# Reordering one attention round across four engines, and the handover from attention to the expert stage

## What is computed

```python
q = layernorm(x) @ Wq + bq;  k = ctx @ Wk + bk;  v = ctx @ Wv + bv      # head width 32, ctx has 722 rows
scores = q @ k.T / sqrt(512)
scores = (scores - mean) / (std(scores, ddof=1) + 1e-8)                # per row
scores = scores + where(mask, -1e-32, 0)
x = x + tanh(g_xattn) * (tile(softmax(scores) @ v, 16) @ Wout + bout)

probs = softmax(layernorm(x) @ router_w.T)                             # 8 experts
weights, indices = top_k(probs, 2);  weights = weights / (weights.sum() + 1e-6)
h = silu(layernorm(x) @ w13[e, :, :1024]) * (layernorm(x) @ w13[e, :, 1024:])
x = x + tanh(g_ffn) * sum_k weights[k] * (h @ w2[indices[k]])
```

## Time and profile before

| what | value |
|---|---|
| median of 3 runs | 438.82 us (436.67 to 439.89) |
| the profiled execution, its own time | 437.29 us |
| its span, first to last instruction | 435.7 us |
| attention, handover: up to the first expert matmul | 131.08 us |
| expert stage and end | 304.6 us |
| mean granted clock of TensorE | 0.928 |

### The profile page before, as it was taken

The page is one execution under the profiler, slowest core; times in us unless marked ns, Lnnn a source line. Parts: engine busy times, 40 slices in busy tenths (PEclk is TensorE's granted clock), DMA queues, the critical chain, the costliest instruction groups (busy, mean ns, idle before and its releaser), DMA issues.

```text
span 435.7 us, 7132 instructions
## 1 busy us (share of the span) xinstructions
PE 372.8 (86%) x1984; PEld 279.5 (64%) x1985; DVE 231.4 (53%) x512; ACT 189.0 (43%) x314; POOL 124.7 (29%) x214
## 2 busy tenths in 40 slices
PE   2979999763009999999899999999999999999990
PEld 2335444441007788888687888888888888888870
DVE  2227777756840277547975135663951873665120
ACT  1124334434621276257863126734752852673120
POOL 2313454454132123130404303133133140431301
PEclk9989889965558999999999999999999999999996
DMA  7977879712019467638898104872772775200201
GB/s 256 364 237 246 303 256 392 241 51 57 0 41 407 180 186 273 214 68 289 306 350 275 36 12 103 287 265 48 270 260 94 227 230 197 48 24 6 48 0 16
DMA packets 17554, 78.01 MB, mean 179 GB/s; under 512 B 3618, under 2 KB 4770, under 8 KB 10372
## 3 DMA queue, kind: packets, MB, share of 16 engines
q1 hardware_dynamic: 11060, 66.79, 43.3%
q0 software_dynamic: 4720, 7.78, 9.0%
q10 hardware_dynamic: 1760, 3.28, 2.3%
HBM read 71.20 MB, written 7.54 MB: 181 GB/s over the span
## 4 chain that ended last, share of the span: by engine, by line
PE 64%; DMA 9%; DVE 8%; issue 7%; POOL 6%; ACT 2%; DVEq 1%; POOLq 1%; ACTq 0%
PE scp L459 19%; PE turnB L439 17%; PE turnA L439 17%; DMA xg<-xn_d,gidx 5%; DMA ent_next<-lists_d 3%; PE kvp L446 3%; PE kvp L308 3%; PE scp L426 2%; POOL lists_d L968 1%; DVE w13l L785 1%; DVE x L749 1%; DVE bn L752 1%; POOL rs L948 1%; PE turnA L294 1%; PE turnA L364 1%
## 5 line engine op out<-in xcount | busy, mean ns | idle before, releaser
L785 DVE TENSOR_TENSOR w13l<-stage,w13h 128x1024 fp32r<-128x1024 f32 x64 | 75.8, 1218 | 3.9 <-ACT w13h L562 3.3
L562 ACT ACTIVATE w13h<-stage 128x1024 fp32r<-128x1024 f32 x64 | 64.5, 1053 | 0.1
L439 PE MATMUL turnA<-w13h,xTh 128*128 128x512 f32 x128 | 51.4, 401 | 1.6 <-DVE xTl L868 1.6
L439 PE MATMUL turnB<-w13h,xTh 128*128 128x512 f32 x128 | 51.9, 405 | 0.0
L459 PE MATMUL scp<-w2h,hTh 128*128 128x512 f32 x128 | 51.8, 404 | 0.0
L439 PE MATMUL turnA<-w13l,xTh 128*128 128x512 f32 x128 | 51.1, 399 | 0.0
L439 PE MATMUL turnA<-w13h,xTl 128*128 128x512 f32 x128 | 51.0, 398 | 0.0
L439 PE MATMUL turnB<-w13l,xTh 128*128 128x512 f32 x128 | 50.5, 395 | 0.0
L439 PE MATMUL turnB<-w13h,xTl 128*128 128x512 f32 x128 | 50.5, 395 | 0.0
L459 PE MATMUL scp<-w2l,hTh 128*128 128x512 f32 x128 | 50.2, 392 | 0.0
L459 PE MATMUL scp<-w2h,hTl 128*128 128x512 f32 x128 | 49.8, 389 | 0.0
(11 more groups left out here) (162 smaller groups left out, 612.7 us busy)
## 6 DMA issues: line engine op xcount, KB each, us to landing
stage<-in_w_dram SPq DMA_DIRECT2D x48, 1024.0 KB, 5.0
ctx_t<-in_ctx_dram SPq DMA_DIRECT2D x8, 1444.0 KB, 8.8
x_t<-in_x_dram SPq DMA_DIRECT2D x8, 200.0 KB
xT_t<-in_xT_dram SPq DMA_DIRECT2D x8, 200.0 KB, 9.6
out_dram<-x ACTq DMA_DIRECT2D x8, 200.0 KB
xn_d<-xn ACTq DMA_DIRECT2D x8, 200.0 KB
stage<-in_wout_dram SPq DMA_DIRECT2D x1, 1024.0 KB, 11.7
ent_next<-lists_d POOLq DMA_DIRECT2D x17, 1.0 KB, 2.0
```

The source lines that it names most:

```text
L439: mm = pe.matmul(region, xp[:, c, :], wp[:, q, c, :], start=(c == 0 and i == 0), stop=(c == HC - 1 and i == 2))
L562: act.activation(dst, src, ACT.Copy).then_inc(S["w_hi"], 1)
L785: dve.tensor_tensor(lo, raw, hi.bitcast(F32), ALU.subtract).then_inc(S["w_lo"], 1)
```

## The change

- ScalarE does the exponential and the four copies for TensorE first in a round. The store of x2, its normalisation and the exponential of the logits come after them.
- The score's standard deviation is made on GpSimd alone, in four operations; the three of VectorE are gone. The sum `taken` also goes from VectorE to GpSimd, and `choose` compares both experts in one operation without the cast. `ltop` gets two buffers.
- On GpSimd the two list scatters of a round stand last, behind `sigma`, and wait for no earlier scatter.
- On VectorE `make_weights` moves one round on, and `ln1_stats` moves ahead of `fix_query`.
- ScalarE and VectorE count `attn_done` ahead of the first 8 splits. VectorE's last split of expert 0 moves behind `x_lo(0)`. GpSimd fetches tile 0 from row 0, without waiting for `tiles_ready` and without reading `tile_row`.
- TensorE gets two waits, in `heads` and in `outputs`, on work of the batch before.

```diff
         ln2 = sb(a, "ln2", [SQ, 2])
         rs2 = sb(a, "rs2", [SQ, 3])
-        ltop = sb(a, "ltop", [SQ, 8])
+        ltop = [sb(a, f"ltop{i}", [SQ, 8]) for i in range(2)]
...
                 pe.wait_ge(S["v_made"], b + 1)
                 pe.wait_ge(S["vsum_set"], b + 1)
                 pe.wait_ge(S["q_fixed"], 2 * min(b + 3, NB))
+                if b >= 1:
+                    pe.wait_ge(S["lg_made"], b)
                 for j in range(KJ):
                     for half in range(2):
...
                 pe.wait_ge(S["head_copied"], b + 1)
                 pe.matmul(l9, headT[:], wx9[:], start=True, stop=True).then_inc(S["low_done"], 1)
                 pe.wait_ge(S["v_made"], min(b + 2, NB))
+                if b >= 1:
+                    pe.wait_ge(S["x2_ready"], b)
                 pe.matmul(outp[0:SQ, :], headT[:], wsum[:], start=True, stop=True).then_inc(S["out_done"], 1)
 
...
 
+            def store_x2(b):
+                act.wait_ge(S["x2_ready"], b + 1)
+                act.dma_start(out[b], x2[b % 2][:]).then_inc(S[f"out_put{b % 2}"], 16)
...
@@ -564,26 +571,22 @@
             for i in ROUNDS:
                 if live(i - 1):
                     softmax_exp(i - 1)
-                if live(i - 2):
-                    act.wait_ge(S["x2_ready"], i - 1)
-                    act.dma_start(out[i - 2], x2[i % 2][:]).then_inc(S[f"out_put{i % 2}"], 16)
                 if live(i):
                     copy_kv(i)
                 if live(i - 1):
                     copy_probT(i - 1)
-                if live(i - 2):
-                    normalise2(i - 2)
-                    logit_exp(i - 2)
-                if live(i - 1):
                     copy_head(i - 1)
                 if live(i + 1):
                     copy_qT(i + 1)
                 if i == 0:
                     wsum_steps()
-                if i == NB + 1:
-                    for unit in range(0, 2 * NQ):
-                        split_hi(0, unit, None)
+                if live(i - 2):
+                    store_x2(i - 2)
+                    normalise2(i - 2)
+                    logit_exp(i - 2)
             act.drain().then_inc(S["attn_done"], 1)
+            for unit in range(0, 2 * NQ):
+                split_hi(0, unit, None)
 
 
             def x_hi(t):
@@ -699,16 +702,6 @@
                 dve.wait_ge(S["sstat"], 2 * (b + 1))
                 dve.bn_aggr(lns[:], bns[:].rearrange("p a b -> p (a b)")).then_inc(S["s_aggr"], 1)
 
-            def finish_sigma(b):
-                dve.wait_ge(S["sig_root"], b + 1)
-                if b >= 1:
-                    dve.wait_ge(S["exp_done"], b)
-                dve.tensor_scalar(sig[:, 3:4], sig[:, 0:1], (SK / (SK - 1)) ** 0.5, SIGMA_EPS, ALU.mult, ALU.add).then_inc(S["sig_sum"], 1)
-                dve.wait_ge(S["sig_sum"], b + 1)
-                dve.reciprocal(sig[:, 1:2], sig[:, 3:4]).then_inc(S["sig_rec"], 1)
-                dve.wait_ge(S["sig_rec"], b + 1)
-                dve.tensor_scalar(sig[:, 2:3], lns[:, 0:1], sig[:, 1:2], -1.0, ALU.mult, ALU.mult).then_inc(S["sig_ready"], 1)
-
             def raw_logits(b):
                 dve.wait_ge(S["low_done"], b + 1)
...
 
             def choose(b):
                 dve.wait_ge(S["lg_made"], b + 1)
-                if b >= 1:
-                    dve.wait_ge(S["lexp_done"], b)
-                    dve.wait_ge(S["nlmax_done"], b)
-                dve.max(ltop[:], lg[b % 2][:]).then_inc(S["lmax_done"], 1)
+                if b >= 2:
+                    dve.wait_ge(S["lexp_done"], b - 1)
+                    dve.wait_ge(S["nlmax_done"], b - 1)
+                dve.max(ltop[b % 2][:], lg[b % 2][:]).then_inc(S["lmax_done"], 1)
                 dve.wait_ge(S["lmax_done"], b + 1)
-                dve.max_index(pidx[:], ltop[:], lg[b % 2][:]).then_inc(S["pidx_done"], 1)
+                dve.max_index(pidx[:], ltop[b % 2][:], lg[b % 2][:]).then_inc(S["pidx_done"], 1)
                 dve.wait_ge(S["pidx_done"], b + 1)
-                dve.tensor_copy(idxf[:], pidx[:, 0:2]).then_inc(S["idx_cast"], 1)
-                dve.wait_ge(S["idx_cast"], b + 1)
                 if b == 0:
                     dve.wait_ge(S["iotas_made"], 1)
-                for k in range(2):
-                    dve.tensor_scalar(hot[:, k, :], e_num[:], idxf[:, k:k + 1], None, ALU.is_equal).then_inc(S["hot_made"], 1)
-                dve.wait_ge(S["hot_made"], 2 * (b + 1))
+                dve.tensor_tensor(hot[:], e_num[:].unsqueeze(1).to_broadcast([SQ, 2, E]),
+                                  pidx[:, 0:2].unsqueeze(2).to_broadcast([SQ, 2, E]), ALU.is_equal).then_inc(S["hot_made"], 1)
+                dve.wait_ge(S["hot_made"], b + 1)
                 if b >= 1:
                     dve.wait_ge(S["rank_done"], b)
+                    dve.wait_ge(S["taken_made"], b + 1)
                 dve.tensor_tensor(both[:], hot[:, 0, :], hot[:, 1, :], ALU.add).then_inc(S["both_made"], 1)
-                dve.wait_ge(S["both_made"], b + 1)
-                dve.wait_ge(S["taken_made"], b + 1)
-                dve.tensor_tensor(taken[:, b + 1, :], taken[:, b, :], both[:], ALU.add).then_inc(S["taken_made"], 1)
 
             def add_attention(b):
@@ -807,11 +796,15 @@
                 if live(i - 2):
                     choose(i - 2)
                     add_attention(i - 2)
+                if live(i - 3) and i <= NB + 1:
+                    make_weights(i - 3)
+                if live(i + 2) and i >= 1:
+                    ln1_stats(i + 2)
                 if live(i + 1):
                     fix_query(i + 1)
                 if live(i):
                     make_values(i)
-                if live(i + 2):
+                if live(i + 2) and i < 1:
                     ln1_stats(i + 2)
                 if live(i):
                     score_stats(i)
@@ -819,14 +812,8 @@
                     wsum_steps()
                 if live(i - 2):
                     make_places(i - 2)
-                    make_weights(i - 2)
                 if live(i - 1):
                     raw_logits(i - 1)
-                if live(i):
-                    finish_sigma(i)
-                if i == NB + 1:
-                    for unit in range(0, 2):
-                        split_lo(0, unit)
 
             dve.wait_ge(S["cnt_done"], 1)
             dve.wait_ge(S["iotas_made"], 1)
@@ -849,10 +836,10 @@
             dve.wait_ge(S["tilerow_done"], 1)
             dve.scalar_tensor_tensor(out=tile_row[:], in0=t_num[0:1, :], scalar=float(P), in1=scp[0:1, 0:TILES],
                                      op0=ALU.mult, op1=ALU.add).then_inc(S["tiles_ready"], 1)
-            for unit in range(2, 2 * NQ):
+            make_weights(NB - 1)
+            dve.drain().then_inc(S["attn_done"], 1)
+            for unit in range(0, 2 * NQ):
                 split_lo(0, unit)
-            dve.drain().then_inc(S["attn_done"], 1)
-
 
 
...
@@ -903,9 +890,9 @@
                 split(6, 7)
                 split(8, 9)
 
-            for unit in (8, 9):
-                split_lo(0, unit)
+            split_lo(0, 8)
             x_lo(0)
+            split_lo(0, 9)
             with dve.Fori(0, E - 1) as e:
                 t0, t1 = tiles_of(dve, e)
...
@@ -949,13 +936,21 @@
                 pool.wait_ge(S["rstd2"], b + 1)
                 pool.tensor_scalar(rs2[:, 1:2], ln2[:, 0:1], rs2[:, 0:1], -1.0, ALU.mult, ALU.mult).then_inc(S["nmean2"], 1)
                 pool.wait_ge(S["lmax_done"], b + 1)
...
+                pool.tensor_scalar(rs2[:, 2:3], ltop[b % 2][:, 0:1], rs2[:, 0:1], -1.0, ALU.mult, ALU.mult).then_inc(S["nlmax_done"], 1)
 
             def sigma(b):
                 pool.wait_ge(S["s_aggr"], b + 1)
                 if b >= 1:
-                    pool.wait_ge(S["sig_sum"], b)
-                pool.tensor_tensor(sig[:, 0:1], lns[:, 1:2], half[:, 1:2], ALU.pow).then_inc(S["sig_root"], 1)
+                    pool.wait_ge(S["exp_done"], b)
+                link(pool.tensor_tensor(sig[:, 0:1], lns[:, 1:2], half[:, 1:2], ALU.pow))
+                link(pool.tensor_scalar(sig[:, 3:4], sig[:, 0:1], (SK / (SK - 1)) ** 0.5, SIGMA_EPS, ALU.mult, ALU.add))
+                link(pool.tensor_tensor(sig[:, 1:2], sig[:, 3:4], half[:, 2:3], ALU.pow))
+                pool.tensor_scalar(sig[:, 2:3], lns[:, 0:1], sig[:, 1:2], -1.0, ALU.mult, ALU.mult).then_inc(S["sig_ready"], 1)
+
+            def count_taken(b):
+                pool.wait_ge(S["both_made"], b + 1)
+                pool.wait_ge(S["taken_made"], b + 1)
+                pool.tensor_tensor(taken[:, b + 1, :], taken[:, b, :], both[:], ALU.add).then_inc(S["taken_made"], 1)
 
             def scatter(b):
...
                 pool.wait_ge(S["lists_set"], 16)
                 for k in range(2):
-                    if b >= 1:
-                        pool.wait_ge(S[f"lists_put{k}"], 16 * b)
                     pool.indirect_dma_start(lists_d, bass.IndirectOffsetOnAxis(place[:, b, k:k + 1], 0),
```

(19 more changed lines are left out.)

8 lines of the change are left out of this document (3 added, 5 removed).

## The result

Before 438.26 us (median of 4 runs, 436.67 to 439.89), changed 422.64 us (median of 4, 421.65 to 423.76): a ratio of 0.9644, 95% interval 0.9594 to 0.9694, faster. The forecast was 422. The profiled execution of the changed kernel took 421.67, its span is 420.1, its mean granted clock 0.948; before it was 437.29, 435.7 and 0.928. The four runs of the changed kernel lie in two pairs, near 421.7 with a mean clock of 0.948 and near 423.7 with 0.936, so a median of a few runs can move by a microsecond without any edit.

The account below looks back on a forecast made before the run. Ahead of the first expert matmul, attention's rounds, the last batch and the handover bound the kernel, with GpSimd narrowly the new bound of a round. Gains of 7.6, 3.1 and 4.8 sum to 15.5: forecast 422 us, range 417.5 to 429.

Parts of the forecast that it names:

- The first matmul carries the end: From the first expert matmul on nothing changes, so the end moves with it: 115.6 in place of 131.08, 15.5 earlier.
- Rounds, 7.6 gained: Attention's five rounds: one of 7.3, then four of 7.6 bound by GpSimd, in place of 9.06; batch 7's projection at 74.9.
- the clock rival: Attention's rounds: TensorE's clock falls low, 450.5 us; chance 0.03 for slower, 0.05 for about half of it, some 436.
- Last batch, 3.1 gained: Batch 7, projection to logits: shorter waits before the exponential and for copies put the logits at 88.3 in place of 98.99.
- To the last scatter: Batch 7's logits to its second list scatter: start at 99.7 in place of 110.87, with 1.2 for contention with VectorE's splits.
- Handover, 4.8 gained to the request: Attention to experts: earlier counts and no table read put tile 0's list request at 104.5 in place of 120.00.
- From the request to the first matmul 11.08 stays: Tile 0's list request to the first expert matmul: the 11.08 us there was to remain unchanged.
- The splits had cover from TensorE: Handover: the weight splits end 4 to 5 us before TensorE would wait for them.
- The rounds give less: Rival, attention's rounds: in-order queue waits make a round 8.6, batch 7's projection 78.9, time 426; chance 0.15.
- The lists landed in 3.15: Rival, handover: lists land late, in 7.8, with dear port and request, 5.7 more, 427.5 us; chance 0.06.
- The lists' waits: List scatters: only one wait for an earlier scatter ever held GpSimd, 2.06, so dropping them alone gives next to nothing.

Follow-up runs that it names:

- sigma_back: The changed kernel with the deviation finished by three small operations on VectorE again, last in its round, after one power on GpSimd: 422.8 us, ratio 0.965.
- hold_gidx: The changed kernel with VectorE's first long split waiting until GpSimd has made the indices of tile 0: 421.28 us, ratio 0.9638.
- splits_last: The changed kernel with both long splits of VectorE moved behind `x_lo(0)`: 420.51 us, ratio 0.9602.
- before_act: The kernel before with ScalarE's new order and TensorE's two waits alone: 439.79 us, ratio 1.0049.

## Why the prediction was right

**The first matmul carries the end.** Right: 15.07 earlier there, 15.62 in the profiled executions, and 304.1 for the rest.

**Rounds, 7.6 gained.** Measured 7.61 between the projections, batch 7's at 74.65 (forecast 74.9). The sum of GpSimd's loop, 7.57, was nearly right: deviation to deviation is 8.06, 7.73, 7.03 and 8.24 where it carries scatters, a mean of 7.77, and sigma_back shows that this loop and not TensorE's makes the last beat, and 7.5 of the one ahead of it. It was not 7.3 and then four of 7.6 but three of 7.3, then 8.03 and 7.70: the exponential came 1.94 after its statistics ahead of the first scatters and 2.70 in the round behind them, so GpSimd's lateness first used up the slack. The 7.61 is closer than it deserves: 0.2 of it is a projection 2 that began at 36.95 and not 37.16 (batch 7's would be 74.86), and with the fourth round at 7.51 the rounds would have been half a microsecond shorter. The scatter pair cost 3.0 to 3.3 with its issue time, forecast 2.85. Statistics to exponential was 2.7 rather than 2.1 in the round shown, because GpSimd was still at `rs` when the statistics came. The lower clock in the old rounds was not named as a source of the gain; it was contained in the 9.06 from which it was counted. The argument against the clock rival, that the clock was low only where TensorE waited for the last batch, was a misreading: it was 0.72 in two stretches of the rounds.

**Last batch, 3.1 gained.** Measured 3.13 (16.52 to 13.39), logits at 88.04 (forecast 88.3). The sum is right and its terms are not: projection to statistics took 7.05 (forecast 6.6), because x and with it the statistics waited for the store of x2, which ScalarE's new order starts late and for which the prediction had no term; the exponential came 1.95 after them (2.05) and the logits 4.39 after that (4.75). That these errors cancel is luck.

**To the last scatter.** Forecast 97.2 and 99.7 for its two starts; measured 97.00 and 98.83, with 1.5 more in the pair's lengths than the 0.99 each of the earlier trace rows. I had taken 1.2 between the ends 0 and 2.3. The rule of the Trainium skill that one of the two blocks the other ("SBUF — State Buffer", Who interferes with whom) agrees with these rows. Its inference that descriptor generation escapes under a `tensor_tensor` does not hold for the indirect DMAs, by the 1.53 and 1.97 here and the gather of 2.49 in hold_gidx against 1.09. For the direct DMA that requests the list it is not contradicted: 0.63 at 104.23, in the middle of the splits, and 0.62 at 120.00 before, between two of them. Whether it is the reading of places and indices that is held up was not tested.

**Handover, 4.8 gained to the request.** Measured 4.82 (logits to request 21.01, then 16.19); the request at 104.23, forecast 104.5. Here too two errors cancel. From the landing of the last scatter to the request the prediction took 0.7, with 1.6 as the dear end; it was 2.25 (101.98 to 104.23), because GpSimd's own drain of 1.38, which was off the chain while VectorE's splits ended last, now stands on it and had no term. Against that the second scatter began 0.87 earlier than forecast and landed in 3.15 in place of 4.1.

**"From the request to the first matmul 11.08 stays"** is the term that was off: 11.78. `gidx` took 2.34 in place of 0.65 and the gather 1.09 in place of 2.19. I had priced VectorE's hold-up on the scatters and not on the two steps behind them, and in the kernel before one of the two, the gather, already had it. The splits had cover from TensorE, as said, but they cost GpSimd: splits_last gives 2.1 back.

**Rivals.** *The rounds give less* needed 41.7 for the five rounds; they took 37.70. Its counter-argument, that the layer norm's inputs are ready before GpSimd comes to them, is not what the trace of before shows (GpSimd waited 3.72 for `ln`). The lists landed in 3.15, below the median of 4.1. The clock did not fall in the rounds. The lists' waits are worth 0.3 by the medians.

**Which part did it.** On the changed kernel, undoing ScalarE's order costs 6.8, the scatters' place 1.0 and the handover 1.0 by the medians, and 7.4, 2.1 and 1.6 by the three columns added up; the lists' waits (0.3 and 0.6) and the variance (0.2 and 0.3) can't be told from nothing. These do not add up to 15.6, and before_act shows why: the parts share their gain, and the largest of them loses alone. What the weights being made a round later is worth by itself was not run.

**Open.** In two rounds results of TensorE were taken up 0.7 to 1 us after the ends that the trace models for its matmuls (around 62 and 77). In hold_gidx, with the same attention code, `probT` and `qn` follow at once around 62 and the round lasts 7.51, so no edit is needed to remove it; what makes it come and go stays open.

## What to carry to other kernels

In a pipelined round, sum each engine's in-order queue for one round, and put first in a queue what the next engine waits for; a reordering can lose alone (0.5% here) and be the largest piece of a combined gain, so look for what stands behind the result that it delays. Where a step of GpSimd is on the chain, look for which long two-input operation of VectorE is running at that moment: moving those behind the chain gave 2.1 us in the column to the first expert matmul, as much as the handover alone (1.9). Count every small step of a chain that is "unchanged", since its neighbours in time have changed, and every wait that was hidden: stores that had always been slow, and a drain that had been off the chain, came onto it here. And check a forecast term by term; here two of its sums were right by errors that cancel.

## What the runs showed of the hardware

- Under VectorE's splits (`tensor_tensor`, both inputs in SBUF), GpSimd's steps grow by about what is left of the split: a `tensor_scalar` on 128x1 from 0.25 to 2.34 when it began 0.04 into a split of 2.29, an indirect gather from 1.09 to 2.49 with 1.51 of the split left. An indirect scatter grew from 0.99 to 1.97. The direct DMA that requests the list took 0.63 in the middle of the splits and 0.62 between two of them. VectorE's splits kept their length (2.29) in the changed kernel and in hold_gidx.
- A drain on GpSimd after the last scatter had landed took 1.38 (with VectorE's splits running), and 0.61 of issue followed ahead of the next DMA.
- While 6 MB of weights were being loaded, stores of x2 took up to 11.1 in the chain of waits (65.65 to 76.75); once those loads were moved behind the rounds, the list scatters became the late ones (6.25 ahead of the request in place of 3.43).
- In attention the granted clock was 0.72 in stretches of 6 with TensorE idle for 0.7 and 0.9 (before), and 1.00 in stretches of 12 and 13 with TensorE idle for 0.1 and 0.8 (changed). It does not follow the idle time of the same stretch alone: from 73 to 82 before it was 1.00 with TensorE idle for 2.0 of 9.
